# Four of sixteen ratio units moved behind the last score of a fused attention kernel

## The reference, cut to what matters

```python
x = x + xattn(layernorm(x), ctx)            # softmax(q k^T / 8) v, 16 heads, 4096 keys
x = x + hyperbolic_attention(layernorm(x))  # below
x = x + experts(layernorm(x))               # gelu(x W1 + b1) W2 + b2, arg-max expert

diff_sq = q_norm_sq + k_norm_sq - 2.0 * qk
denom = maximum((1 - q_norm_sq) * (1 - k_norm_sq), 1e-06)
cosh_arg = maximum(1.0 + 2.0 * diff_sq / denom, 1.0)
attn = softmax(-arccosh(cosh_arg))
```

## Time and profile before

| | us |
|---|---|
| median of 3 runs | 1109.94 |
| lowest, highest | 1108.46, 1110.03 |
| profiled execution, its own time | 1110.04 |
| its span in the profile | 1108.3 |
| mean granted TensorE clock, share of 2.4 GHz | 0.972 |

### The profile page before, as it was taken

One profiled execution on the slowest core, in us unless ns is written; L12 is line 12 of the kernel. 1 busy time (PEld: TensorE's weight loads), 2 busy tenths in 40 slices (PEclk: granted clock), 3 DMA queues, 4 the chain that ended last, 5 costly groups with the idle time before them and its releaser, 6 DMA issues.

```text
span 1108.3 us, 36598 instructions
## 1 busy us (share of the span) xinstructions
PE 1042.3 (94%) x15401; PEld 779.7 (70%) x15401; DVE 811.8 (73%) x1061; ACT 793.3 (72%) x1452; POOL 667.9 (60%) x611
## 2 busy tenths in 40 slices
PE   6799999999999999999999999999999999667888
PEld 3476777777777777777777777777767777543466
DVE  5988887777777777777777777767777759548442
ACT  6587777777777777777777777777777756699754
POOL 6365666666666666666666666676664556833033
PEclk9999999999999999999999999999999999786699
DMA  7920420000000000000000000003000010000000
GB/s 232 243 45 16 73 45 7 16 7 17 7 17 7 17 7 17 7 16 8 16 7 17 7 17 7 17 7 121 7 3 7 26 54 3 2 1 1 1 1 20
DMA packets 50932, 31.73 MB, mean 29 GB/s; under 512 B 27194, under 2 KB 47698, under 8 KB 50770
## 3 DMA queue, kind: packets, MB, share of 16 engines
q1 hardware_dynamic: 50770, 29.39, 10.2%
HBM read 22.57 MB, written 0.52 MB: 21 GB/s over the span
## 4 chain that ended last, share of the span: by engine, by line
PE 81%; DVE 6%; ACT 5%; issue 4%; POOL 2%; DMA 1%; SPq 0%; ACTq 0%; POOLq 0%; DVEq 0%
PE ps L1461 15%; PE ps L1406 14%; PE ps L1543 14%; PE ps L1490 6%; PE ps L1589 5%; PE ps L1584 5%; PE ps L1587 5%; PE ps L1531 5%; PE ps L815 2%; PE ps L775 2%; POOL psums L2144 2%; PE ps L1522 1%; PE ps L1391 1%; PE ps L591 1%; DVE m_part L1951 1%
## 5 line engine op out<-in xcount | busy, mean ns | idle before, releaser
L2144 POOL TENSOR_TENSOR psums<-probs 128x512 f16<-128x512 f32 x512 | 590.8, 1174 | 327.2 <-ACT probs L1785 273.5
L1776 ACT ACTIVATE probs<-ps 128x512 f32<-128x512 f32 x512 | 279.7, 600 | 193.0 <-PE ps L1543 192.1
L1951 DVE TENSOR_REDUCE m_part<-ps 128x2 f32<-128x1024 f32 x256 | 312.7, 1224 | 135.9 <-PE ps L1490 134.6
L1785 ACT ACTIVATE probs<-probs 128x512 f16<-128x512 f32 x384 | 242.1, 632 | 0.3
L1543 PE MATMUL ps<-q_hi,k_p 64*128 64x256 f16 x2048 | 211.2, 269 | 0.0
L1584 PE MATMUL ps<-v_sb,probs 128*128 128x65 f16 x2048 | 205.3, 192 | 4.5 <-POOL psums L2144 4.5
L1587 PE MATMUL ps<-v_sb,probs 128*128 128x64 f16 x2048 | 205.3, 192 | 0.0
L1589 PE MATMUL ps<-v_sb,psums 128*128 128x65 f16 x2048 | 204.9, 194 | 0.0
L1584 PEld LDWEIGHTS ps<-v_sb,probs 128*128 128x128 f16 x2048 | 188.3, 98 | 19.6 <-POOL psums L2144 6.1
L1587 PEld LDWEIGHTS ps<-v_sb,probs 128*128 128x128 f16 x2048 | 188.0, 97 | 16.1
L1589 PEld LDWEIGHTS ps<-v_sb,psums 128*128 128x128 f16 x2048 | 188.2, 97 | 0.0
(11 more groups left out here) (249 smaller groups left out, 1670.6 us busy)
## 6 DMA issues: line engine op xcount, KB each, us to landing
ctx_hi<-in_L_ffn_W_dram SPq DMA_DIRECT2D x2, 2048.0 KB, 10.6
probs<-in_ctx_dram SPq DMA_DIRECT2D x4, 512.0 KB, 7.0
wqk_raw<-in_L_xattn_w_q_dram SPq DMA_DIRECT2D x16, 128.0 KB, 2.3
wqk_raw<-in_L_xattn_w_k_dram SPq DMA_DIRECT2D x16, 128.0 KB, 2.6
k_p<-in_ctx_dram SPq DMA_DIRECT2D x4, 512.0 KB, 11.2
wv_raw<-in_L_xattn_w_v_dram SPq DMA_DIRECT2D x16, 128.0 KB, 2.5
wo_raw<-in_L_xattn_w_o_dram SPq DMA_DIRECT2D x16, 128.0 KB, 2.1
ctx_hi<-in_ctx_dram SPq DMA_DIRECT2D x7, 256.0 KB, 5.8
```

Of the source, the lines that this page charges most:

```text
L1776: nc.scalar.activation(p_raw[:, s:s + 2, h, :], ps[:, score_bank(n, pair, h), :].rearrange("p (k q) -> p k q", k=2), ACT.Exp, scale=XSCALE ...
L1785: nc.scalar.activation(p_hi[:, s % NP, :, :], p_raw[:, s % NX, :, :], ACT.Copy) \
L1951: nc.vector.tensor_reduce(m_part[:, j, t, :], ps[:, bank:bank + 2, :], AX.X, ALU.max) \
L2144: nc.gpsimd.tensor_tensor(p_lo[:, s % NP, :, :].rearrange("p h q -> p (h q)"), p_raw[:, s % NX, :, :].rearrange("p h q -> p (h q)"), p_hi[ ...
```

## The change

`UNIT_AT` keeps its first twelve units, at slots 10 to 21. Units 12 to 15 leave slots 22 to 25 on TensorE and on VectorE. On TensorE each now stands ahead of `pv` of one of the slots 28 to 31, behind the last score. On VectorE their `ratios` stand behind the whole of `last_step` and ahead of `take_output` of the last step. No operation is added or removed. Lines of `kernel.py` move by 1 below line 83, by 5 below the loop on TensorE and by 7 at the end.

```diff
-UNIT_AT = {10 + u: u for u in range(16)}
+UNITS_BEFORE = 12
+UNIT_AT = {10 + u: u for u in range(UNITS_BEFORE)}
@@ tensor
             last_step(STEPS - 1)
+            late = list(enumerate(attn_units()[UNITS_BEFORE:16]))
             for s in range(SLOTS - 4, SLOTS):
+                for u, (m, gg, _, i, kt, jj) in late:
+                    if u * 4 // len(late) == s - (SLOTS - 4):
+                        distances(pe, m, 0, i, kt, jj)
                 pv((STEPS - 1) * SLOTS + s, s, STEPS - 1)
@@ vector
             last_step(STEPS - 1)
+            for m, gg, _, i, kt, jj in attn_units()[UNITS_BEFORE:16]:
+                ratios(dve, m, gg, 0, kt, jj)
             take_output(STEPS - 1, STEPS * SLOTS - 1)
```

## The result

The changed kernel takes 1116.16 us (median of 4 runs, 1115.72 to 1118.21) where the kernel before takes 1109.72 (4 runs). The ratio is 1.0063, with a 95% interval of 1.0049 to 1.0077. That is slower by 6.4 us and lies outside the range of the prediction, 1108.4 to 1112.6.

The account below looks back on a forecast made before the run. GpSimd and its turns with VectorE were taken to bound the last step's end. Copy +0.9, slot 31 0 and clock -0.2 give +0.7 us: 1110.04 becomes 1110.7 us, bounds 1110.0 to 1111.4, 8-in-10 range 1108.4 to 1112.6.

Parts of the forecast that it names:

- the chain behind the copy: From the output copy on, work is serial: L1522 waits 0.52 us and L591 0.69 us for the engine before.
- the turns of VectorE and GpSimd: Last step: both engines alternate on operations with data in SBUF; each turn costs GpSimd about 0.9 us.
- the copy +0.9: Last step's output copy on VectorE starts at 956.6 against 955.73, +0.9 us, bounds +0.5 and +1.3.
- the units chain: Rival: TensorE issues each late unit only after VectorE's last one; 2.4 us more, copy at 959.0, 1113.2 us; chance 0.03.
- the bound by TensorE: Copy start: unit 15 ready between 954.9 and 955.4, its two operations take 1.4 us, so copy at 956.3 to 956.8.
- Three hide in waits for GpSimd: TensorE, last four products: three of the four late units, 0.54 us each, fit into waiting for GpSimd.
- The bound by VectorE's queue: Copy start: last L880 ends up to 0.7 us before 951.55, 5.35 us follow, so copy between 956.2 and 956.9.
- the 950.9 to 951.6 that I had named as a sign: Sign that the forecast is right: VectorE's last L880, a low part of the expert weight, ends at 950.9 to 951.6.
- The end of slot 31: GpSimd's last slot of the last step: end taken as unchanged, between 0.4 us earlier and 0.6 us later.
- the term of -0.2: TensorE's clock before L1522: a fifth of 0.97 us won, 0.2 us; bounds 2.5 won or 1.5 lost.
- clock high: Rival: TensorE's clock stays high; L1522 and L591 at 1.00 win 2.5 us, 1108.4 us; chance 0.17.
- The rival in which the low level lasts longer: TensorE's clock returns to 1.00 one block later behind L591: price 1.5 us, 1112.8 us; chance 0.15.

Follow-up runs that it names:

- The kernel with narrow low parts: Kernel before with the last step's four low parts (L880) cut to 8 of 1024 columns, the rest left out: 1106.03 us, ratio 0.997.
- the kernel with GpSimd's wait: Changed kernel, with GpSimd's first ratio addition waiting until the last step's normalisation is done: 1109.83 us, ratio 1.0012 against the kernel before.
- ten reciprocals and the wait: Kernel before with ten 128x4 reciprocals ahead of the last normalisation, and GpSimd's first addition waiting for that normalisation: 1108.77 us, ratio 0.9998.
- the version with the addition behind the layer norm: Kernel before, low parts of quarters 6 and 7 behind the last normalisation, GpSimd's first addition waiting for them and batch 1's layer norm: 1106.42 us, ratio 0.9976.

## Why the prediction was wrong

**The step that failed** is in the paragraph on the chain behind the copy: "what the copy loses reaches the end unless a later wait absorbs it". I took the chain as serial and passed a delay through it one for one. I had stated the turns of VectorE and GpSimd from the earlier trace rows, and used them only inside the step, on the low halves. The next operation of VectorE behind the copy, the normalisation, has both inputs in SBUF, and GpSimd's longest operation starts 0.51 us behind it. What decides is by how much more the normalisation is delayed than the addition. My own numbers had that: the copy +0.9, the product of slot 31, on which the addition hangs, +0.1 to +0.6. From a lead of 0.51 that leaves 0.51 - 0.9 + 0.35 = -0.04 us, so the order was a toss-up within my own bounds. On the bad side of it, with an end 0.28 us behind the addition (a figure that only the runs gave), the normalisation ends at 957.26 + 4.51 + 0.28 = 962.05 and not at 957.72, and the time is 1110.7 + 4.3 = 1115.0. A rival of that price with about half of the chance was missing. Of the rivals that I had, the units that chain came nearest with 1113.2, by a mechanism that did not happen: TensorE nowhere waits for L1137 ahead of a late unit.

The Trainium skill states the rule, in "SBUF — State Buffer", section "SBUF: two separate sides": VectorE and GpSimd share a port pair under an exclusive lock that is held for a whole instruction, and a VectorE operation with two SBUF inputs contends for it against a GpSimd operation that reads SBUF. The trace agrees: 4.72 us behind an addition that started 0.05 us earlier, 0.42 ahead of it.

**The copy, +0.9 forecast, +1.58 measured.** The term that was mis-sized is the bound by TensorE. I had the product of slot 30 start at its old time; corrected, it starts at 954.13 instead of 953.74, since unit 14 and its own predecessor stand ahead of it. It then takes 0.77 us and not 0.6, and unit 15 takes 0.97, inside my 0.54 to 1.08 but above its middle. Unit 15 so ends at 955.87 and not between 954.9 and 955.4, and the copy follows 1.44 us later. "Three hide in waits for GpSimd" was wrong: only the product behind unit 12 still waited for GpSimd, and VectorE waited 0.93, 0.32 and 0.32 us for L664 ahead of the other three units. The first of these waits comes from a turn that moved. In before, TensorE's long wait for GpSimd is at the product of slot 29:

```profile
952.62 0.24 PE L1584 MATMUL ps<-v_sb,probs 128*128 128x65 f16 x1 [1.55 <-POOL psums L2144]
```

In after the last low part stands earlier, and it is slot 28 of GpSimd that takes its turn with it, so the product of slot 28 starts 0.60 us later than before's (951.13, corrected, against 950.53), and unit 13 stands behind it. From there to the last product TensorE waits for nothing: at the low clock a product and a unit take 1.74 us together (955.19 to 956.93), where GpSimd needs 1.15 for a slot. The bound by VectorE's queue was not wrong but did not bind: the last low part ended 1.5 us sooner (951.12, corrected 950.06, against 951.55), where I had allowed 0.7, and outside the 950.9 to 951.6 that I had named as a sign.

**The end of slot 31, 0.4 earlier to 0.6 later**: right. It ended at 68.28 from the zero against 68.64, so the 0.36 us of GpSimd's idle time were won, and no more. The exponentials of pair 13 started 0.74 us sooner (943.52, corrected 942.46, against 943.20) without effect, as said. The kernel with narrow low parts shows that the reason, the turns, was right as well.

**The clock.** I gave -0.2 for the way to the output projection. L1523 took 2.08 us as before, so nothing came there. The eight query rows took 3.18 us instead of 3.58, but that is no gain: the two matmuls of L602 behind them took 1.06 us instead of 0.60, and from the start of the eight to that of the four are 4.38 us instead of 4.28. So the term of -0.2 came out as +0.1 here, and what the clock did give, most of the 1.3 us of the account, fell in the experts, where I had no term. The change of level that I had as a rival (clock high, 1.5 us on L591) is real and shows in the kernel with GpSimd's wait, 1.99 us, but not in after. The rival in which the low level lasts longer did not come about: the four behind took 1.03 us.

**Which signs I had named**: the copy at 956.3 to 956.9 was to be right, and it came at 957.31 corrected. This one sign would have said that TensorE was at fault. No sign I named looked at the normalisation.

**What stays open.** What decides the clock at the query rows. From the start of the eight to the start of the four behind them are 2.69 to 2.70 us in six of the profiled runs, where the eight take 1.99, and 4.28 to 4.38 us in six others, however that time is split between the eight (3.2 to 3.7) and what follows; in one, with ten reciprocals and the wait, it is 5.28. I found no order in this by start or by the stretch before. The 1.06 us ahead of the zero were not traced to anything either; in the kernel with the wait, which has the same change, it is -0.12, and in one without the change +1.66, so it is no trait of the change.

## What to carry to other kernels

Before letting a delay pass one for one through a chain, look for each operation that shares a resource with another engine, and note by how much it now comes first. A small operation that leads a long one by half a microsecond stands at a cliff: if it loses less than its lead, it costs that much, and if it loses more, nearly the long one's whole length. Where such a lead is found, a wait on the long operation's side makes the order certain, for nothing if that engine has time. And work laid into idle time beside the last output must be checked on the engine that produces for it, at the clock it has there: here the idle time was VectorE's, but the units had to come from TensorE at its lower level.

## What the runs showed of the hardware

That a VectorE operation waits for a GpSimd operation of 4.5 us to its end was new to me; the longest hold in the earlier trace rows was 2.14 - 1.15 = 1 us. It does not hold for all of them. Beside the running addition, 128x4 reciprocals went through at about 0.07 us each (five between 957.56 and 957.91, behind an addition that started at 957.51), two statistics of 128x256 took 0.75 us, the same as in the version with the addition behind the layer norm, and an operation on 128x2 from SBUF to SBUF was held for 1.67 us. What in the form of an instruction decides that was not tried. Operations that read PSUM were not held: the units' eight operations took 0.69 us each, beside GpSimd's subtractions and without them, and in the kernel with the last two low parts behind the normalisation an addition of 128x512 with one input in PSUM took 0.69 us beside the 4.5 us addition, as without it. The output copy stood beside a long GpSimd operation in no run.
